# Attention over 1,601 keys: the keys of the batch after next are summed and split one key tile sooner and transposed one tile later, and the transposition of x waits for one partial maximum less

## The reference

```
q_big  = rope(einsum('bshk,hkq->bshq', (x @ Wq.T) per head, w_kc_q))      # 64 queries, 16 heads
kv_r   = rope(ctx_512)                                                    # 32 batches, 1601 keys of 64
scores = einsum(q_big . W_qr, kv_r . W_kr)                                # per batch 1024 columns (head, query)
attn   = softmax(scores over the 1601 keys)
x     += (attn @ kv_r, through w_kc_kv and Wo)
```

## Time and profile before

| | before |
|---|---|
| median of three runs | 2978.64 us |
| profiled execution: device time | 2975.01 us |
| its span | 2973.2 us |
| TensorE busy in the span | 2699.5 us (91%) |
| GpSimd busy in the span | 1241.8 us (42%) |
| TensorE's mean granted clock | 0.966 |

### The profile page before, as it was taken

The page is one execution under the profiler, slowest core; times in us unless marked ns, Lnnn a source line. Parts: engine busy times, 40 slices in busy tenths (PEclk is TensorE's granted clock), DMA queues, the critical chain, the costliest instruction groups (busy, mean ns, idle before and its releaser), DMA issues. The chain is left out here.

```text
span 2973.2 us, 46845 instructions
## 1 busy us (share of the span) xinstructions
PE 2699.5 (91%) x16984; PEld 1662.9 (56%) x16984; DVE 1524.8 (51%) x2432; ACT 1146.7 (39%) x2192; POOL 1241.8 (42%) x664
## 2 busy tenths in 40 slices
PE   6969567999999999999999999999959799999999
PEld 4656345555655665565556556656436465656555
DVE  4746685464555446455544655564349633332322
ACT  3647463344434344443444453354425311111110
POOL 1011013577667667766766776676700000000000
PEclk9989698999999999999999999999979899999999
DMA  1000401111101011110101111010040000000000
GB/s 46 0 17 0 153 1 52 46 41 45 40 28 56 28 45 40 45 37 31 56 28 45 40 45 40 28 56 21 13 197 0 1 1 7 1 8 0 1 7 8
DMA packets 27084, 100.34 MB, mean 34 GB/s; under 512 B 3904, under 2 KB 8640, under 8 KB 25216
## 3 DMA queue, kind: packets, MB, share of 16 engines
q1 hardware_dynamic: 25632, 97.60, 9.9%
q10 hardware_dynamic: 1376, 1.71, 0.2%
HBM read 57.68 MB, written 2.10 MB: 20 GB/s over the span
## 5 line engine op out<-in xcount | busy, mean ns | idle before, releaser
L736 POOL TENSOR_TENSOR cx_acc<-cx_acc,cx_prob 128x1024 f32<-128x1024 f32 (+1 forms) x352 | 835.0, 2372 | 369.9 <-ACT cx_prob L1027 357.3
L1027 ACT ACTIVATE cx_prob<-cx_st 128x512 f32<-128x512 f32 (+1 forms) x832 | 474.0, 595 | 428.4 <-PE cx_st L868 416.1
L1131 DVE TENSOR_REDUCE cx_mhalf<-cx_mx 128x1 f32<-128x804 f32 x512 | 482.9, 989 | 225.8 <-PE cx_mx L844 225.6
L879 PE MATMUL cx_av<-cx_prob,cx_kv 128*64 128x512 f32 (+1 forms) x1664 | 449.1, 618 | 0.0
L867 PE MATMUL cx_st<-cx_q,cx_k 128*128 128x512 f32 (+1 forms) x832 | 370.3, 445 | 7.9 <-ACT cx_prob L1027 7.3
L868 PE MATMUL cx_st<-cx_q,cx_k 128*128 128x512 f32 (+1 forms) x832 | 331.0, 398 | 0.0
L844 PE MATMUL cx_mx<-cx_kp,cx_q 128*128 128x402 f32 x1024 | 299.9, 379 | 19.5 <-DVE cx_mhalf L1131 18.2
L844 PEld LDWEIGHTS cx_mx<-cx_kp,cx_q 128*128 128x128 f32 x1024 | 171.5, 191 | 202.0 <-DVE cx_mhalf L1131 183.7
L1857 ACT ACTIVATE moe_silu<-moe_gate 128x512 f32<-128x512 f32 x112 | 66.9, 597 | 521.4 <-PE moe_gate L1765 521.4
L867 PEld LDWEIGHTS cx_st<-cx_q,cx_k 128*128 128x128 f32 (+1 forms) x832 | 156.8, 188 | 183.7 <-ACT cx_prob L1027 140.0
L1109 DVE TENSOR_TENSOR cx_turn<-cx_mx,cx_tab 128x384 f32<-128x384 f32 x256 | 130.9, 553 | 241.7 <-PE cx_mx L802 241.7
(11 more groups left out here) (217 smaller groups left out, 3670.9 us busy)
## 6 DMA issues: line engine op xcount, KB each, us to landing
cx_k<-cx_kp SPq DMA_DIRECT2D x32, 804.0 KB, 3.9
cx_ctx<-in_cx_ctxN SPq DMA_DIRECT2D x32, 416.0 KB, 3.2
cx_ctxr<-in_cx_ctxrN SPq DMA_DIRECT2D x32, 416.0 KB, 3.9
cx_k<-cx_kp SPq DMA_DIRECT2D x32, 402.0 KB, 5.2
moe_wgu<-in_moe_wgu SPq DMA_DIRECT2D x7, 1024.0 KB, 13.1
moe_wd<-in_moe_wd SPq DMA_DIRECT2D x4, 896.0 KB, 24.1
x_all<-in_x SPq DMA_DIRECT2D x1, 2048.0 KB, 6.4
f_w<-in_f_w SPq DMA_DIRECT2D x2, 1024.0 KB, 6.0
```

What stands on the lines that cost most here:

```text
L736: pool.tensor_tensor(acc[rows, :, :], sofar, prob[slot(kt)][rows, :, :], ALU.add).then_inc(s_acc, 1)
L879: last = pe.matmul(av[DCX * p:DCX * p + DCX, :], kv[e][0:nk(kt), kt, :], prob[slot(kt)][0:nk(kt), p, :], start=(kt == 0), stop=(kt == NKT ...
L1027: act.activation(prob[slot(kt)][rows, p, :], st[p][rows, :], ACT.Exp).then_inc(s_exp, 1)
L1131: dve.tensor_reduce(mhalf[:, i // 2, i % 2:i % 2 + 1], mx[i % 2][:, :, 0:KQ], AX.XY, ALU.max)\
```

## The change

Five numbers of the table move, and the wait ahead of the transposition of x is for one reduction less; the reduction left out is waited for by the second of the big queries.

```diff
-    KV_AT = 3
+    KV_AT = 2
     OUT_AT = 5
-    SUM_AT = 4
-    KH_AT = 6
-    KL_AT = 7
-    TURN_AT = 7
+    SUM_AT = 3
+    KH_AT = 5
+    KL_AT = 6
+    TURN_AT = 8
...
                 if not is_first(t):
-                    pe.wait_ge(s_mr, 2 * t * PIECES)
+                    pe.wait_ge(s_mr, 2 * t * PIECES - 1)
                 for c in range(DC):
                     last = pe.transpose(mx[0][:, 0, c * P:(c + 1) * P], xn[:, c * P:(c + 1) * P], ident[:, :])
...
             def big(t, j):
                 if j == 0:
                     pe.wait_ge(s_xTc, t + 1)
+                if j == 1 and not is_first(t):
+                    pe.wait_ge(s_mr, 2 * t * PIECES)
```

## The result

The changed kernel takes 2924.64 us in the median (2922.98 to 2932.56, 4 runs), the kernel before 2977.49 beside it. The ratio is 0.9828, with a 95% interval of 0.9811 to 0.9845: some 51 us are gained. Beside later experiments the same kernel gave 0.9833 (0.9808 to 0.9858). The forecast was 2913 us, with a range of 2901 to 2938; it promised 12 us too many. The time alone would not tell which of its steps failed: 2925 is also what the rival gives by which the clock falls stay, and 2927 the one by which GpSimd is the new bound. The batches inside the loop tell them apart.

What follows compares the result with a forecast made beforehand. TensorE, busy nine tenths or more in the long attention, was the bound; only its idle time or clock pays. 37.6 - 1.4 + 16.4 + 11.7 = 64.3 us off 2975.0 gives 2910.7, forecast as 2913 for the median; range 2901 to 2938.

Steps and rivals of the forecast that it cites:

- the clock falls stay: Rival, 15%: TensorE's clock still falls in odd batches, or falls come elsewhere; 2925 us.
- GpSimd is the new bound: Rival, 9%: GpSimd costs more, another 1 us remaining in each of 14 odd batches; 2927 us.
- The wait for the remainder goes, 37.6 us: Odd batches: TensorE's key transposition no longer waits for GpSimd's remainder, 15 waits, 37.6 us in all.
- The remainder sooner and the transposition later: Odd batches: GpSimd's remainder ends one add earlier, near 717.07; TensorE's transposition moves one key tile later.
- The wait for x, 16.4 us: TensorE's transposition of x: the whole 1.09 us wait for VectorE's reduction of `mx[1]` goes, 16.4 us in all.
- The clock, 11.7 us: Odd batches: with the long wait gone, TensorE's clock falls in seven batches go too, gaining 11.7 us.
- GpSimd just about the bound, -1.4 us: Odd batches: TensorE wants the sum as GpSimd ends; 0.1 us lost in each of 14, bounds 0 and 0.6.
- The bound by GpSimd's own work, 36.99 us: Odd batches, GpSimd's first add to end of twelfth: 39.07 us less its waits, so no end before 735.66.
- for engines that now come sooner: GpSimd's chain in odd batches: its waits of 0.45 and 1.63 us were left out of its own work.
- What stretches is VectorE's normalisation, and nobody on the path waits for it.: Argument against the slower rival: beside GpSimd's add VectorE's normalisation takes 2442 ns, not 406; adds stay 2333 to 2403.
- ScalarE at no price: ScalarE's moved copy of the values and rounding fit within cover of 0.15 and 0.8 us: price zero.
- The rival of a slower kernel: Rival, 3%: GpSimd's instructions lengthen when run without pause beside VectorE; decides from 4.3 us a batch, 2985 at 5.

Runs made afterwards that it cites:

- the table alone: The kernel before with only the five numbers of the table changed and the wait for x left whole: 2942.52 us, ratio 0.9852.
- the transposition alone: The changed kernel with only TURN_AT moved (7 to 8), the table's other four numbers as before the change: 2927.7 us, ratio 0.9827.
- the variance sooner: The changed kernel with VectorE's statistics and variance for the next x put ahead of the last four reductions: 2918.47 us, ratio 0.9766.

## Why the prediction was right in direction and too large in size

Between the first and the last odd batch (the 15 odd and 14 even lengths), the profiles give 622.7 and 590.0 us for the odd batches and 870.1 and 851.9 for the even ones: 32.7 and 18.2 us, 50.9 in all. The forecast's terms for this stretch are 47.9 and 15.3 (14 of the 15 waits for x), 63.2. The 12.3 us between them are, to within 0.3, the 15.5 that GpSimd's bound cost more than forecast, less the 2.9 that the wait for x gave back more. Its steps:

- *The wait for the remainder goes, 37.6 us.* Right, and shown by the changed kernel, by the table alone and by the transposition alone. In the last odd batch, where no rotation and no root are laid into GpSimd's program, the length is 37.83 us against 42.46 in the earlier trace rows.
- *The remainder sooner and the transposition later.* The prediction presents the two moves as one. Each alone is enough, but for 0.08 us a batch. Its own numbers had this and it didn't say so: one add sooner, the remainder ends at 717.07, when TensorE comes free; and left at 719.49, it is still ahead of a transposition asked for near 720.3.
- *The wait for x, 16.4 us.* Right in mechanism, a little small: 1.3 us for each even batch, not 1.09. The row gives idle time from the end that the profile models for the last matmul. With no wait, the transposition begins 0.16 us ahead of that end in all 15 cases, which makes 1.25 of the 1.30; 14 x 1.3 = 18.2.
- *The clock, 11.7 us.* Right: no odd or even batch of the changed kernel's loop has a fall, and with the wait left in they return. The rival that they stay or come elsewhere, at 15%, is refuted.
- *GpSimd just about the bound, -1.4 us.* This is the step that failed, and the rival of 9% is what happened: 16.9 us in the place of 1.4. The bound by GpSimd's own work, 36.99 us, was sound: with the variance sooner it goes from its first add to the end of its twelfth in 37.05 us, and odd batches of 38.4 us were measured, inside the forecast 38.2 to 38.5. What was wrong is the line that its waits of 0.45 and 1.63 us were "for engines that now come sooner". VectorE did come sooner: its cast begins 28.7 us after the denominators where it began 31.8 us after them. But so it came to stand at the start of an add, and of the 3.1 us gained the variance kept only 0.8. GpSimd's wait for it shrank from 1.63 to 1.12 us and didn't go.
- *"What stretches is VectorE's normalisation, and nobody on the path waits for it."* showed VectorE held up beside an add, 2442 ns instead of 406, and I drew from it only that GpSimd doesn't pay. It does when it waits for an instruction that stands behind the one held up. The Trainium skill says in "GPSIMD Engine Reference", section "1. Specifications", that the two share their SBUF interfaces, with contention for VectorE's two-port modes and for two SBUF inputs. For two inputs the trace agrees: 2.23 us for the subtraction. The cast, 2.41 us, has one input, and whether it ran in a two-port mode no trace tells.
- *ScalarE at no price.* Right: TensorE's waits for the exponentials are 3.5 us over the whole kernel (L869) in the changed profile and were 7.3 us (L867) before.
- *"At 5 us it is 2925 + 60 = 2985."* The rival of a slower kernel doesn't say where 2925 and 60 come from; 5 us in each of 14 batches on 2913 is 2983. Nothing hangs on it: GpSimd's adds didn't get longer.

## What to carry to other kernels

When a wait is removed, list the waits of the engine that is second near its limit, and ask for each not only whether its releaser comes sooner, but what stands in front of the releaser and beside what that will now run. In this kernel a short VectorE cast within SBUF, or a subtraction of two tensors there, took until the end of the GpSimd add beside it. So nothing that GpSimd itself waits for should stand behind such an instruction, or GpSimd should ask for it one instruction later. And where each of two moves clears the same wait, make one and measure: here the second bought nothing that the times could tell.

## What the runs showed of the hardware

- VectorE's cast of 128x8 took 0.17 us alone and up to 2.41 beside an add of GpSimd; a subtraction of 128x8 with two SBUF inputs took 0.17 alone and 2.20 to 2.24 beside the add that had begun 0.17 us before it. Each ended within 0.05 us of the add. A reduction of 128x8 in SBUF took 0.16 to 0.17 beside an add. GpSimd's adds to the running sum kept between 2.33 and 2.46 us in every kernel.
- The same 2.5 us wait of TensorE brought a fall of the granted clock from 1.00 in 7 of 15 batches in one kernel and in 11 of 15 in another whose even batches were 1.3 us shorter; a fall cost 1.3 to 2.8 us a batch. Waits of 1.1 to 1.3 us brought none, in 15 even batches before and 14 odd batches after the change.
